# Scaling quantised pairs back on GpSimd instead of VectorE, with two unit buffers

## The reference

```python
def fp4_quant_dequant(x):             # blocks of 16 along the last dim
    scale = jnp.max(jnp.abs(xb), axis=-1, keepdims=True) / 6.0
    scale = jnp.maximum(scale, jnp.float32(1e-12))
    xn = xb / scale
    idx = jnp.searchsorted(_MID, jnp.abs(xn))
    q = _GRID[idx] * jnp.sign(xn) * scale
...
gate = fp4_linear(x, w_gate)
y = fp4_linear(x, w_up)
h = jax.nn.silu(gate) * y             # 352 wide
return fp4_linear(h, w_down)
```

## Time and profile before

| | |
|---|---|
| runs | 692.53, 693.09, 696.05 us |
| median | 693.09 us |
| profiled execution | 695.96 us |
| its span, first to last instruction | 694.2 us |
| mean granted TensorE clock | 0.984 |

### The profile page before, as it was taken

How to read it: one execution, slowest core, us unless ns; L and a number is a source line. 1 busy time by engine, 2 the same in 40 slices (tenths; PEclk the granted TensorE clock), 3 DMA queues, 4 the chain that set the end, 5 groups by cost and what they waited for, 6 DMA issues and landing times.

```text
span 694.2 us, 10228 instructions
## 1 busy us (share of the span) xinstructions
PE 645.5 (93%) x3585; PEld 469.7 (68%) x3599; DVE 463.7 (67%) x1082; ACT 440.9 (64%) x826; POOL 181.4 (26%) x217
## 2 busy tenths in 40 slices
PE   5889999999998999998999999998889998989997
PEld 2679996566666766776677667865556665757775
DVE  3586675687658376378667685376976763767775
ACT  5576454977567748676458486555346855978773
POOL 3433000631232141232431512032013500004521
PEclk9999999999999999999999999999999999999999
DMA  5220002030002010202020020010000300000001
GB/s 143 55 74 23 1 1 77 1 93 1 1 15 76 4 43 0 77 1 91 17 76 1 28 64 2 0 49 0 2 1 1 112 13 0 1 1 30 1 1 30
DMA packets 27361, 20.98 MB, mean 30 GB/s; under 512 B 5409, under 2 KB 22571, under 8 KB 27311
## 3 DMA queue, kind: packets, MB, share of 16 engines
q1 hardware_dynamic: 26591, 20.29, 9.6%
q10 hardware_dynamic: 720, 0.04, 0.1%
HBM read 19.80 MB, written 0.52 MB: 29 GB/s over the span
## 4 chain that ended last, share of the span: by engine, by line
PE 65%; ACT 14%; DVE 14%; issue 4%; POOL 2%; DMA 1%; SPq 0%; DVEq 0%; POOLq 0%; ACTq 0%
PE PS L1637 56%; ACT PS L905 4%; PE PS L1905 3%; ACT H1h L903 2%; ACT H2h L903 2%; PE PS L1762 2%; ACT XN L807 2%; DVE H2l L1282 2%; DVE H1l L1282 1%; PE PS L1927 1%; POOL RSTD L687 1%; ACT ATT L791 1%; PE PS L1815 1%; PE PS L1658 1%; ACT WH L791 1%
## 5 line engine op out<-in xcount | busy, mean ns | idle before, releaser
L1282 DVE TENSOR_TENSOR H2l<-PS,H2h 128x512 fp32r<-128x512 f32 x104 | 70.8, 689 | 70.3 <-ACT PS L905 69.1
L695 POOL TENSOR_TENSOR WL<-RAW,WH 128x512 fp32r<-128x512 f32 (+2 forms) x76 | 86.1, 1149 | 107.6 <-ACT WH L791 107.4
L1282 DVE TENSOR_TENSOR H1l<-PS,H1h 128x512 fp32r<-128x512 f32 x80 | 54.3, 689 | 29.9 <-ACT PS L905 29.1
L713 POOL TENSOR_TENSOR XT<-XT,YW 128x512 f32<-128x512 f32 x24 | 31.0, 1292 | 142.0 <-DVE YW L1219 141.8
L687 POOL TENSOR_TENSOR RSTD<-VE,MHALF 128x4 f32<-128x4 f32 x18 | 19.5, 1086 | 173.4 <-DVE VE L1109 137.7
L791 ACT ACTIVATE ATT<-PS 77x512 f32<-77x512 f32 (+6 forms) x92 | 46.8, 532 | 27.3 <-PE PS L1905 11.5
L1637 PE MATMUL PS<-H1h,WH 128*128 128x512 f32 x146 | 60.7, 416 | 2.3 <-DVE H1l L1282 2.3
L1637 PE MATMUL PS<-MB,identb 128*128 128x512 bf16 (+1 forms) x228 | 57.3, 372 | 2.0 <-DVE H1l L1282 0.8
L1637 PE MATMUL PS<-H1l,WH 128*128 128x512 f32 x146 | 57.5, 394 | 0.0
L1637 PE MATMUL PS<-H1h,WL 128*128 128x512 f32 x146 | 57.3, 393 | 0.0
L1637 PE MATMUL PS<-XTh,WH 128*128 128x512 f32 x128 | 52.9, 413 | 2.8 <-POOL WL L695 2.0
(11 more groups left out here) (267 smaller groups left out, 1593.0 us busy)
## 6 DMA issues: line engine op xcount, KB each, us to landing
RAW<-in_L_ffn_spec_W SPq DMA_DIRECT2D x4, 1024.0 KB, 5.5
RAW<-in_L_ffn_w SPq DMA_DIRECT2D x16, 256.0 KB, 3.0
RAW<-in_L_ffn_up_W SPq DMA_DIRECT2D x8, 256.0 KB, 2.6
RAW<-in_L_ffn_down_W SPq DMA_DIRECT2D x8, 256.0 KB, 3.2
RAW<-in_L_ffn_spec1a_W SPq DMA_DIRECT2D x2, 512.0 KB, 4.1
RAW<-in_L_ffn_spec1b_W SPq DMA_DIRECT2D x2, 512.0 KB, 5.7
RAW<-in_L_ffn_wg SPq DMA_DIRECT2D x4, 176.0 KB, 2.8
RAW<-in_L_ffn_wu SPq DMA_DIRECT2D x4, 176.0 KB, 3.0
```

Source lines behind the costliest of these rows:

```text
L695: g.tensor_tensor(lo, RAW[0:r["rows"], r["raw"] + s["c0"]:r["raw"] + s["c1"]], hi.bitcast(fp32), ALU.subtract).then_inc(lo_done, 1)
L713: g.tensor_tensor(y, y, YW[:, (d % 2) * HALF:(d % 2 + 1) * HALF], ALU.add).then_inc(y_added, 1)
L1282: v.tensor_tensor(lo, full, hi.bitcast(fp32), ALU.subtract).then_inc(split_done, 1)
```

## The change

The multiply that scales a rounded pair back to its blocks moves from VectorE to GpSimd (scaled_pair). GpSimd does pairs 0 and 1 between the norm steps 13 and 14, pairs 2 and 3 between the steps 14 and 15. Each waits for a new semaphore, rounded_ready, which VectorE raises with the last rounding instruction, and from pair 1 on for the turn of the pair before. The factor -1 of the old instruction goes into the units' constant, so that QA holds the negated units. The units alternate between two buffers, QAP, since GpSimd may still be reading one pair's while VectorE writes the next one's. VectorE gets a new wait: gated_pair(p) for p = 2, 3 waits, ahead of its block maxima, until GpSimd is done with pair p-2, whose scale table it overwrites. One semaphore is freed by folding heads_ready into const_copied, which now counts to three.

```diff
+        QAP = [QA, ATT3[:, 768:768 + 2 * I2]]
...
+            def scaled_pair(p):
...
+                scale = QSP[p % 2][:, 0, 0:nb].rearrange("p (b o) -> p b o", o=1).to_broadcast([128, nb, QB])
+                pool.wait_ge(rounded_ready, p + 1)
+                if p >= 1:
+                    pool.wait_ge(f2_t, 2 * p)
+                g.tensor_tensor(blk(HQ), blk(QAP[p % 2]), scale, ALU.mult).then_inc(f2_q, 1)
...
-            rstd(12, 13, 14, 15)
+            rstd(12, 13)
+            scaled_pair(0)
+            scaled_pair(1)
+            rstd(14)
+            scaled_pair(2)
+            scaled_pair(3)
+            rstd(15)
...
-                s.activation(QC, QA, ACT.Abs, scale=MAGIC).then_inc(size_ready, 1)
+                s.activation(QC, QAP[p % 2], ACT.Abs, scale=MAGIC).then_inc(size_ready, 1)
...
-            v.tensor_reduce(HG4[:, :], HM[:, :].rearrange("p (g m) -> p m g", g=NG), AX.X, ALU.max).then_inc(heads_ready, 1)
+            v.tensor_reduce(HG4[:, :], HM[:, :].rearrange("p (g m) -> p m g", g=NG), AX.X, ALU.max).then_inc(const_copied, 1)
...
                 dve.wait_ge(f2_used, 2 * p + 2)
+                if p >= 2:
+                    dve.wait_ge(f2_q, p - 1)
...
-                v.scalar_tensor_tensor(blk(QA), blk(QD[:, 0:2 * I2]), 1.0 - 2.0 ** -23, per,
+                v.scalar_tensor_tensor(blk(QAP[p % 2]), blk(QD[:, 0:2 * I2]), 2.0 ** -23 - 1.0, per,
...
-                now(v.scalar_tensor_tensor(QA, QC, 1.5 * MAGIC, QA, ALU.max, ALU.add))
-                now(v.scalar_tensor_tensor(QA, QC, 1.5 * MAGIC, QA, ALU.max, ALU.subtract))
-                if p >= 1:
-                    dve.wait_ge(f2_t, 2 * p)
-                v.scalar_tensor_tensor(blk(HQ), blk(QA), -1.0, scale, ALU.mult, ALU.mult).then_inc(f2_q, 1)
-                dve.wait_ge(f2_q, p + 1)
+                now(v.scalar_tensor_tensor(q, QC, 1.5 * MAGIC, q, ALU.max, ALU.add))
+                v.scalar_tensor_tensor(q, QC, 1.5 * MAGIC, q, ALU.max, ALU.subtract).then_inc(rounded_ready, 1)
+                dve.wait_ge(rounded_ready, p + 1)
```

More of the change, by code:

```diff
@@ L519, in program @@
         pt_full, pt_act, pt_dve, o_full, o_done = sem("pt_full"), sem("pt_act"), sem("pt_dve"), sem("o_full"), sem("o_done")
-        heads_ready = sem("heads_ready")
         ot_ready, back_full = sem("ot_ready"), sem("back_full")
@@ L531, in program @@
         act_high = sem("act_high")
-        unit_ready, size_ready = sem("unit_ready"), sem("size_ready")
+        unit_ready, size_ready, rounded_ready = sem("unit_ready"), sem("size_ready"), sem("rounded_ready")
         ring_full, act_freed, dve_freed = sem("ring_full"), sem("act_freed"), sem("dve_freed")
@@ L717, in prepare @@
                     low_part(s)
+            def scaled_pair(p):
+                blk = lambda x: x.rearrange("p (b k) -> p b k", k=QB)
+                nb = 2 * I2 // QB
+                scale = QSP[p % 2][:, 0, 0:nb].rearrange("p (b o) -> p b o", o=1).to_broadcast([128, nb, QB])
[3 more added lines that the diff above has]
+                g.tensor_tensor(blk(HQ), blk(QAP[p % 2]), scale, ALU.mult).then_inc(f2_q, 1)
             def head_keys(layer, kt, some):
                 if layer == 1 and 0 in some:
-                    pool.wait_ge(heads_ready, 1)
+                    pool.wait_ge(const_copied, 2)
                 for b in some:
@@ L1532, in _ @@
             v.tensor_scalar(MB1[:, :], MI[:, :], 0.0, MASKED, ALU.is_equal, ALU.mult).then_inc(const_copied, 1)
-            dve.wait_ge(const_copied, 2)
+            dve.wait_ge(const_copied, 3)
             for i in range(2):
@@ L1601, in rounded @@
             def rounded(p):
-                blk = lambda x: x.rearrange("p (b k) -> p b k", k=QB)
-                nb = 2 * I2 // QB
-                scale = QSP[p % 2][:, 0, 0:nb].rearrange("p (b o) -> p b o", o=1).to_broadcast([128, nb, QB])
+                q = QAP[p % 2]
                 dve.wait_ge(size_ready, p + 1)
-                now(v.scalar_tensor_tensor(QA, QC, 1.5 * MAGIC, QA, ALU.max, ALU.add))
-                now(v.scalar_tensor_tensor(QA, QC, 1.5 * MAGIC, QA, ALU.max, ALU.subtract))
-                if p >= 1:
-                    dve.wait_ge(f2_t, 2 * p)
-                v.scalar_tensor_tensor(blk(HQ), blk(QA), -1.0, scale, ALU.mult, ALU.mult).then_inc(f2_q, 1)
-                dve.wait_ge(f2_q, p + 1)
+                now(v.scalar_tensor_tensor(q, QC, 1.5 * MAGIC, q, ALU.max, ALU.add))
+                v.scalar_tensor_tensor(q, QC, 1.5 * MAGIC, q, ALU.max, ALU.subtract).then_inc(rounded_ready, 1)
+                dve.wait_ge(rounded_ready, p + 1)
             gated_pair(0)
@@ L2049, in _ @@
                 mm(PS[i][0:R0, :], Wu[:, :], XT[:, i * HALF:(i + 1) * HALF]).then_inc(a0_up, 1)
-            pe.wait_ge(const_copied, 2)
+            pe.wait_ge(const_copied, 3)
             pe.wait_ge(a0_upc, 2)
```

## The result

| | before | changed |
|---|---|---|
| median, executions of both beside each other | 695.54 us (7) | 698.65 us (7) |
| profiled execution: time, span | 695.96, 694.2 us | 697.61, 695.9 us |
| ratio, 95% interval | | 1.0051 (1.0031 to 1.0071) |

The changed kernel came out 0.5% slower (the ratio is of the means, the medians give 0.45%), and its median lies 0.45 us above the range that I had given. Measured three more times, each time beside the kernel before, it gave 1.0059, 1.0017 and 1.0008. The mean of the four is 1.0034. The intervals of the single ratios alone would put 0.0011 on either side of it, but the four lie further apart than these intervals allow for; by their own scatter the mean is worth about 0.004 on either side. So the totals leave the size of the loss open, and what follows rests on a stretch inside the profile.

What follows compares the result with a forecast made beforehand. VectorE was on the path only before 499.2 and from 508.28 to about 513.4 us, with TensorE's written order between. Terms +0.7 and +1.1 (+1.8) plus +1.2 for the clock gave +3.0: 693.09 to 696.1 us, range 693.2 to 698.2.

Steps and rivals of the forecast that it cites:

- What VectorE gains: Four scaling multiplies, 3.7 us in all, leave VectorE; the freed time only lengthens waits, is replaced or falls into slack.
- Price of the multiply: GpSimd's 128x704 multiply takes 1.5 us, kept at 1.36 to 1.70, against VectorE's 0.89.
- rival (d): Multiply priced by its 44 short blocks, decisive from 1.75 us; at 2.1 us +4.2, 697.3 us; chance 0.15.
- Who blocks whom: VectorE's units start first and block GpSimd's multiply in pairs 0 to 2, adding up to 0.7 us.
- (b): No blocking, the multiply runs beside units at 1.5 us; +0.5, no clock drop, 693.6 us; chance 0.10.
- (c): GpSimd gets in first and units wait for it; +1.6, with the clock drop +2.8, 695.9 us; chance 0.08.
- First term: Pair 0: late HQ delays TensorE's turn and up2(3), 499.9 against 499.23; +0.7 us.
- Second term: Pair 2: late HQ delays its turn by 1.33 us more, less 0.25 of ScalarE slack; +1.1 us.
- Cover of pairs 1 and 3: HQ of these pairs is ready before TensorE asks, hidden by 0.8 and 0.5 us.
- Third term, the clock: TensorE's 2.26 us idle before pair 2's turn drops the granted clock to 0.5; between 0 and 1.7, taken +1.2 us.
- Rival (a): The clock holds behind the idle before pair 2's turn; +1.8, 694.9 us; chance 0.22.
- The total: Whole kernel +3.0 us on the median 693.09, giving 696.1 us, +0.43%; chance 0.45.

Runs made afterwards that it cites:

- e4: Changed kernel with the units' reciprocals in PSUM; layer (first block maximum to next attention's first scores) 40.01 us against 39.91 before, ratio 1.0001.
- e1: Kernel before with GpSimd scaling back pairs 0 and 1 only, VectorE pairs 2 and 3; layer 40.33 us, +0.42, ratio 1.0011.
- e2: Kernel before with GpSimd scaling back pair 2 only, VectorE the other three; layer 40.99 us, +1.08, ratio 1.0022.
- e3: Kernel before with GpSimd scaling back pair 3 only; layer 39.92 us against 39.91 before, ratio 1.0003.
- e6: Changed kernel with every GpSimd multiply done twice; layer 46.63 us, +6.7 against the kernel before, ratio 1.0124.
- e8: Changed kernel with pair 2 rounded before line 1362's sum and its GpSimd multiply ahead of norm step 14; layer 40.29 us, ratio 1.0016 against the kernel before.
- null: Kernel before, unchanged, measured against itself; layer 39.91 us, ratio 1.0000 (0.9979 to 1.0020).

## Why the prediction was right or wrong

- **What VectorE gains: nothing.** Right. Its idle before line 1362's sum grew from 0.77 to 2.09 us.
- **Price of the multiply.** 1.38 us, at the lower bound of 1.36 from the block keys; I took 1.5. The 44 short blocks cost 0.02 at most, and rival (d) falls with it. The estimate of 1.75 from the factor 1.96 of the Trainium skill (GPSIMD Engine Reference, section Performance versus the Vector engine) lies too high; against VectorE's 0.89 the measured factor is 1.55. One operand repeated in place seems to be what makes it cheaper, but only the two kinds of rows say so.
- **Who blocks whom.** Right in direction and size: I had 0.7 us on top, measured 0.65 to 0.71; units lost nothing; e4 took it away. Rivals (b) and (c) fall. The Trainium skill's rule (SBUF — State Buffer, section Who interferes with whom) holds in the two parts that were tried: units with two SBUF operands hold GpSimd's multiply up (2.03 to 2.09 us), with one in PSUM they don't (e4, 1.38 and 1.39).
- **First term** +0.7, measured +0.37 in the changed kernel (its L1362 sum, 30.10 us into the layer against 29.73) and 0.42 in e1. Mis-sized: 0.12 by the multiply, the rest by the handover to up2(3), which came 0.71 behind the turn's start and not 0.8, and by up2(3) itself running 0.1 shorter without waits inside.
- **Second term** +1.1, measured +1.08 (e2). Partly luck: at the measured 1.38 my working gives 0.96. The missing 0.1 is in small pieces: the turn came 1.25 later and not 1.21, ScalarE's slack gave 0.21 and not 0.25, and the copies to the scores took 0.03 longer.
- **Cover of pairs 1 and 3**: right, both turns without a wait; HQ was there 0.47 and 0.68 us ahead of them, where I had 0.8 and 0.5. e3 shows pair 3's by itself.
- **Third term, the clock: wrong.** This is the step that failed. I had read three idle stretches of 1.89 us and more, all followed by a fall, as if such a stretch were enough. Five profiles with 2.18 or 2.19 us here kept the full clock; so did e6 behind 2.63, and not behind 3.64. The three stretches that I had read it from don't bear it out either: behind the one of 2.50 us the clock fell in only half of the twenty profiles (last section). The term was 0 where I took +1.2. Rival (a), at +1.8 on my multiply and +1.5 on the measured one, is what happened in the layer: +1.44.
- **The total.** The forecast of +3.0 and the measured +3.1 agree by accident: 1.44 are in the layer, and the rest lies outside it, where two of three repeats have nothing like it (1.0017, 1.0008; the third has 1.0059). By the profiles, what differs outside the layer is where the clock falls; for the executions that make up the medians, which have no trace, that it was the clock is not shown. The absent third term would have brought the time down; that it came out above the range has to do with this rest and with the base. I had put the sum on the median of three executions, 693.09, as if that were the kernel's; seven gave 695.54, and later ones 693.47 to 695.38. A median that can move by 2 us had no place in my bounds: the range was made of the mechanisms alone. With the layer's +1.44 on 695.54 the time would have been 697.0, inside it.

## What to carry to other kernels

Before work is given to GpSimd, look at what VectorE runs just behind it: if that has two SBUF operands, the true price is GpSimd's own time plus most of the VectorE instruction (here 0.65 to 0.71 of 0.89 us). Moving one operand to PSUM gives it back (1.34 of 1.44 us in e4), and so does an order in which VectorE next runs something with one operand in PSUM (in e8 pair 2's multiply, beside line 1362's sum, took 1.39 us). Freed time on an engine is worth something only if the order of the others lets it through, so find the queue that asks for the result and count when it asks. Where executions scatter by several microseconds for a reason of their own, measure a fixed stretch inside the profile, run the kernel against itself, and put the scatter of the baseline into the range.

## What the runs showed of the hardware that I had not expected

The falls of the granted clock differ between executions of one kernel: the full-clock work lost, added up over stretches of five microseconds, was 10.2 us in the first profile of the kernel before and 5.5 in the second, and 5.1 to 8.5 in four of the changed one, mostly in steps of about 1.7. That is more than the whole change. The scatter of the totals goes with it. Of 148 executions of the kernel before, the 25 with a mean granted clock of 0.990 or more took 692.1 us on average, the 64 with 0.984 or less 695.8.

The same idle stretch of TensorE was followed by a fall in one execution and not in another. In the first profile of the kernel before the 2.50 us ahead of 217.46 were followed by one, in the second (null) they weren't. The stretch of the first; TensorE's timeline of the second and its stretch (us, busy, count, granted clock, DMA share, GB/s):

```profile
215.00:220.00 5.00, 2.54 (x10) 0.75 0.74 246
...
215.93 1.09 PE L1815 MATMUL PS<-ident,SN 128*128 128x128 f32 x8 [2.50 <-DVE SN L1240]
215.00:220.00 5.00, 4.07 (x26) 1.00 0.49 175
```

Over the twenty profiles of all kernels here, the clock fell at or behind this idle of 2.50 us in ten, behind the one of 2.0 near 318 us in all twenty, behind the one of 1.89 near 575 in eighteen (not in e2 and not in the changed kernel's fourth), and behind 2.18 in the layer in none of five. The length of an idle stretch alone doesn't tell. The time behind the layer goes with the one near 575: 174.2 to 174.3 us without a fall, 175.7 to 175.9 with a shorter one, and 176.8 to 177.1 where the clock was at 0.5 for the whole five microseconds behind that idle.

And GpSimd's multiply with one operand repeated innermost in blocks of 16 runs at (1.38 - 0.19) / 704 = 1.69 ns a column, where its plain two-operand instructions take 2.14.
